# A node table stored twice with a mate mark, a shorter search, a later bias and a fuller tail in a four-layer graph kernel

## What is computed

```python
x = x + gnn0(layernorm(x), adj)      # bilinear attention in each graph, masked by adj, then elu
x = x + ffn0(layernorm(x))           # top-1 of 8 experts, 128 -> 512 -> 128, with a capacity per expert
x = x + gnn1(layernorm(x), adj)      # additive attention in each graph, out = attn @ hidden + bias
x = x + ffn1(layernorm(x), edges)    # GAT over the edges picks 2 of 4 experts per token
```

```python
h = (x_flat @ W_gat).reshape(M, HEADS, NUM_EXPERTS)       # 16 numbers per node
a_src, a_dst = (h * att_src).sum(-1), (h * att_dst).sum(-1)
e = leaky_relu(a_src[src] + a_dst[dst])                   # one loop edge per node is added
alpha = softmax of e over the edges that end in dst
agg = segment_sum(h[src] * alpha, dst)                    # 16 numbers per node
scores = layernorm(agg + b).mean over heads; the two best of 4 gelu experts, weighted, give the result
```

## Time and profile before

| | us |
|---|---|
| three runs of the kernel | 3044.87, 3047.87, 3049.06 (median 3047.87) |
| profiled execution, its own time | 3049.74 |
| its span (first to last instruction) | 3047.3 |

### The profile page before, as it was taken

One profiled execution on the slowest core, in us unless ns is written; L12 is line 12 of the kernel. 1 busy time (PEld: TensorE's weight loads), 2 busy tenths in 40 slices (PEclk: granted clock), 3 DMA queues, 4 the chain that ended last, 5 costly groups with the idle time before them and its releaser, 6 DMA issues. The chain is left out here.

```text
span 3047.3 us, 31102 instructions
## 1 busy us (share of the span) xinstructions
PE 1772.2 (58%) x8831; PEld 1216.7 (40%) x8831; DVE 2258.0 (74%) x4431; ACT 1155.4 (38%) x2319; POOL 1867.5 (61%) x1723
## 2 busy tenths in 40 slices
PE   0776774068787883566963356455545554555545
PEld 0565653045555552355761133233323332333223
DVE  7999998889999999777843655665566556655566
ACT  2676773234444441365941222222222222222222
POOL 4703244835454553477767777777777777777771
PEclk9998895589999997688956677677777777777777
DMA  5698000111111100222121122112211222122211
GB/s 217 210 354 323 16 23 15 33 38 35 35 44 42 53 27 35 71 58 69 34 41 29 39 45 43 33 41 45 43 37 36 45 43 41 35 43 45 43 31 36
DMA packets 170129, 192.34 MB, mean 63 GB/s; under 512 B 59241, under 2 KB 126096, under 8 KB 169008
## 3 DMA queue, kind: packets, MB, share of 16 engines
q1 hardware_dynamic: 107616, 118.69, 11.7%
q0 software_dynamic: 57088, 62.48, 10.1%
q10 hardware_dynamic: 5328, 9.97, 0.9%
HBM read 91.70 MB, written 105.25 MB: 65 GB/s over the span
## 5 line engine op out<-in xcount | busy, mean ns | idle before, releaser
L1582 POOL DMA_INDIRECT edge_rows<-node_table,edge_ids x1024 | 999.3, 976 | 313.2 <-issue 296.5
L1207 POOL DMA_INDIRECT token_results<-arena,token_of x160 | 255.4, 1596 | 293.4 <-ACT arena L1141 220.7
L634 DVE TENSOR_TENSOR sort_ping<-sort_pong 128x1024 f32<-128x1024 f32 (+1 forms) x232 | 395.2, 1745 | 6.0 <-ACT sort_pong L1077 1.1
L634 DVE TENSOR_TENSOR sort_pong<-sort_ping 128x1024 f32<-128x1024 f32 (+1 forms) x230 | 390.2, 1738 | 10.9 <-ACT sort_ping L1077 6.0
L1705 PE MATMUL x_b_featT<-ident,x_feat 128*128 128x128 f32 x128 | 34.8, 427 | 620.1 <-PEq L1304 620.1
L1200 POOL DMA_INDIRECT slots<-arena,send x128 | 190.0, 1485 | 301.9 <-ACT arena L1099 268.0
L1452 DVE TENSOR_TENSOR win_score<-win,masked 128x320 f32<-128x320 f32 x64 | 28.7, 490 | 446.3 <-DMA win<-edge_table,win_ids 445.1
L1711 PE MATMUL x_b_hid<-x_featT,x_w 128*128 128x512 f32 x512 | 312.2, 765 | 28.1 <-PEq L1304 28.1
L1718 PEld LDWEIGHTS x_b_res<-x_w,x_hid 128*128 128x128 f32 x2048 | 247.0, 197 | 97.5 <-issue 97.5
L1705 PEld LDWEIGHTS x_b_featT<-ident,x_feat 128*128 128x128 f32 x128 | 22.9, 217 | 625.4 <-issue 625.4
L1718 PE MATMUL x_b_res<-x_w,x_hid 128*128 128x128 f32 x2048 | 272.1, 288 | 0.0
(11 more groups left out here) (367 smaller groups left out, 4060.7 us busy)
## 6 DMA issues: line engine op xcount, KB each, us to landing
edge_table<-zeros SPq DMA_DIRECT2D x8, 5120.0 KB, 36.0
edge_rows<-node_table,edge_ids POOLq DMA_INDIRECT x1024
arena<-slots SPq DMA_DIRECT2D x40, 260.0 KB, 2.6
slots<-zeros SPq DMA_DIRECT2D x2, 5120.0 KB, 24.4
edge_table<-edge_rows SPq DMA_DIRECT2D x64, 160.0 KB, 2.1
out_dram<-x_y ACTq DMA_DIRECT2D x33, 256.0 KB, 4.1
x<-in_x_dram SPq DMA_DIRECT2D x4, 2048.0 KB, 16.7
adjacent<-in_adj_dram SPq DMA_DIRECT2D x32, 256.0 KB, 2.7
```

The source lines that it names most:

```text
L634: step(dve.tensor_tensor(vb[:, :, t, :], va[:, :, 0, :], va[:, :, 1, :], op))
L1207: pool.indirect_dma_start(rows_dram, bass.IndirectOffsetOnAxis(token_of[:, n % 4, r:r + 1], 0), res[:, n % 2, r, :], None, bounds_check=TO ...
L1582: pool.indirect_dma_start(rows[:, u, c, :], None, table_dram, bass.IndirectOffsetOnAxis(ids[:, u, c:c + 1], 0)).then_inc(rows_in[u], 16)
```

## The change

1. **Node table twice.** `node_table` has 2 x 16384 rows of 21 floats (`EDGE_ROW`; 84 B) in place of 16384 rows of 24 (96 B). Column 20 (`MATE_AT`) is 0 in the first copy and 1 in the second; it is filled, row by row, by two DMAs of SP behind the clears, which write whole rows of `zeros` and of a new tile `second_row`. The ids of the edges' sources keep the mate bit of the key (mask `MATES * NODE_BIT - 1`), so that an edge of the second mate fetches its source's row from the second copy, and carries the mark into `edge_table` (now 21 floats a row, cleared in pieces of 672 floats).
2. **The store of the table.** Each of the four stores L961 becomes two, one per copy, of 128 x 32 x 20 floats; SP waits for eight.
3. **A quarter of the search goes.** Of 32 searches, the 8 that looked up the second mate's first edge are left out (`SEARCHED`): 192 instead of 256 indirect DMAs on POOL, 24 instead of 32 pairs of operations on DVE. The 24 stand where the loop's 24 stood before; the searches behind the loop are gone. What is left of either mate's run is now counted from the pair's first edge (`pair_degree`).
4. **Hiding by the mark.** In each of the 32 turns the single operation on `hide` (L1458) becomes two on as many elements (a maximum, and a comparison with a maximum) that read the mark from the window.
5. **Later bias.** `dve_biased` stands at the head of GNN1's iteration, for n+2, where it stood behind the scores, for n+3.
6. **Fuller tail.** The condition on `advance()` in the tail of GNN0 goes, so the iterations 34, 36 and 38 take one step of the sort each, too.

```diff
+MATE_AT = ROW
+EDGE_ROW = ROW + 1
...
+CLEAR_EDGES = 32 * EDGE_ROW
...
-        zeros = sb("zeros", [P, CLEAR])
+        zeros, second_row = sb("zeros", [P, CLEAR_EDGES]), sb("second_row", [P, EDGE_ROW])
...
+        EACH = ALL_PAIRS // SEARCH
+        SEARCHED = [n for n in range(SEARCHES // SEARCH) if n // EACH != 2]
...
                     place(LAST_OF.index(n - 2))
-                if n <= GROUPS + 1 or n % 2:
-                    advance(2 if n > GATED and n % 2 == 0 and n <= GROUPS else 1)
+                advance(2 if n > GATED and n % 2 == 0 and n <= GROUPS else 1)
                 att0.dve_updated(dve, n - 1)
...
-                cols = slice(n * SEARCH, (n + 1) * SEARCH)
+                cols = slice(SEARCHED[n] * SEARCH, (SEARCHED[n] + 1) * SEARCH)
...
             for n in range(-3, GROUPS + 1):
+                att1.dve_biased(dve, n + 2)
                 att1.dve_held(dve, n - 1)
                 att1.dve_scores(dve, n + 2)
-                att1.dve_biased(dve, n + 3)
                 att1.dve_updated(dve, n - 1)
...
-                    link(dve.tensor_scalar(tiles_u, table[:, :].bitcast(U32), NODE_BIT - 1, None, ALU.bitwise_and))
+                    link(dve.tensor_scalar(tiles_u, table[:, :].bitcast(U32), MATES * NODE_BIT - 1, None, ALU.bitwise_and))
...
             for n in range(GROUPS + 1 - LAG, GROUPS):
                 gat.dve(dve, n)
-                if n % 3 == 0:
-                    search()
-            while searched[0] < SEARCHES // SEARCH:
+            while searched[0] < len(SEARCHED):
                 search()
...
-            clear(sp, edges_dram, cleared)
+            clear(sp, edges_dram, cleared, CLEAR_EDGES)
...
+            for mate, row in enumerate((zeros[:, 0:EDGE_ROW], second_row[:, :])):
+                copy_v = table_dram[mate * TOKENS:(mate + 1) * TOKENS, :].rearrange("(p r) c -> p r c", p=P)
+                sp.dma_start(copy_v, row.unsqueeze(1).to_broadcast([P, GRAPHS, EDGE_ROW])).then_inc(cleared, 16)
...
                 sp.wait_ge(gat.kept, (c + 1) * CHUNK)
-                sp.dma_start(table_v[:, cols, :], tab[:, cols, :]).then_inc(tabled, 16)
-            sp.wait_ge(tabled, 16 * (GROUPS // CHUNK))
+                for mate in range(MATES):
+                    sp.dma_start(table_v[mate][:, cols, 0:ROW], tab[:, cols, 0:ROW]).then_inc(tabled, 16)
+            sp.wait_ge(tabled, 16 * MATES * (GROUPS // CHUNK))
...
-            link(dve.tensor_tensor(by_mate(left[:, 0:GRAPHS], 0), by_unit(second_of[:, 0:ALL_PAIRS]), by_unit(first_edge), ALU.subtract))
-            link(dve.tensor_copy(by_mate(left[:, 0:GRAPHS], 1), by_unit(pair_degree[:, :])))
+            for mate in range(MATES):
+                link(dve.tensor_copy(by_mate(left[:, 0:GRAPHS], mate), by_unit(pair_degree[:, :])))
...
+            second = w[:, :, :, MATE_AT]
...
-                step(dve.scalar_tensor_tensor(hide[:, PAIRS:UNIT, :], hide[:, PAIRS:UNIT, :], 1.0, hide[:, 0:PAIRS, :], ALU.add, ALU.subtract))
+                step(dve.tensor_tensor(hide[:, 0:PAIRS, :], hide[:, 0:PAIRS, :], second, ALU.max))
+                step(dve.scalar_tensor_tensor(hide[:, PAIRS:UNIT, :], second, 0.5, hide[:, PAIRS:UNIT, :], ALU.is_lt, ALU.max))
...
-    table_dram = nc.dram_tensor("node_table", (TOKENS, TAB), F32).ap()
+    table_dram = nc.dram_tensor("node_table", (MATES * TOKENS, EDGE_ROW), F32).ap()
...
-    edges_dram = nc.dram_tensor("edge_table", (BLOCKS_MAX * BLOCK, ROW), F32).ap()
+    edges_dram = nc.dram_tensor("edge_table", (BLOCKS_MAX * BLOCK, EDGE_ROW), F32).ap()
```

More of the change, by code:

```diff
@@ L595, in front, with clears, clear @@
                      (spread_a, NODE_BIT << 16), (spread_b, 3 * NODE_BIT << LOG_NODES))
-        def clears(table):
-            return -(-(math.prod(table.shape) // P) // (CLEAR * REPEAT))
-        def clear(sp, table, done):
+        def clears(table, run=CLEAR):
+            return -(-(math.prod(table.shape) // P) // (run * REPEAT))
+        def clear(sp, table, done, run=CLEAR):
             flat = table.rearrange("(p r) d -> p (r d)", p=P)
-            width = math.gcd(flat.shape[1], CLEAR)
-            for c in range(clears(table)):
-                part = flat[:, c * CLEAR * REPEAT:min((c + 1) * CLEAR * REPEAT, flat.shape[1])].rearrange("p (r w) -> p r w", w=width)
+            width = math.gcd(flat.shape[1], run)
+            for c in range(clears(table, run)):
+                part = flat[:, c * run * REPEAT:min((c + 1) * run * REPEAT, flat.shape[1])].rearrange("p (r w) -> p r w", w=width)
                 sp.dma_start(part, zeros[:, 0:width].unsqueeze(1).to_broadcast(list(part.shape))).then_inc(done, 16)
@@ L931, in _ @@
                 sp.dma_start(adjacent[:, c % ADJ_SLOTS, :], a["adj"][:, c * WIDE:(c + 1) * WIDE]).then_inc(adj_in[c % ADJ_SLOTS], 16)
-            sp.wait_ge(zeroed, 1)
+            sp.wait_ge(zeroed, 3)
             clear(sp, slots_dram, slots_clear)
             clear(sp, rows_dram, unwritten)
-            clear(sp, edges_dram, cleared)
+            clear(sp, edges_dram, cleared, CLEAR_EDGES)
             ids_tail = ids_dram[P:, :].rearrange("r (p f) -> (r p) f", f=4 * PART_TILES)
             sp.dma_start(ids_tail, zeros[:, 0:4 * PART_TILES].bitcast(U32)).then_inc(cleared, 16)
+            for mate, row in enumerate((zeros[:, 0:EDGE_ROW], second_row[:, :])):
+                copy_v = table_dram[mate * TOKENS:(mate + 1) * TOKENS, :].rearrange("(p r) c -> p r c", p=P)
+                sp.dma_start(copy_v, row.unsqueeze(1).to_broadcast([P, GRAPHS, EDGE_ROW])).then_inc(cleared, 16)
             for s in sent:
@@ L955, in _ @@
             sp.wait_ge(ids_out, 16)
-            sp.wait_ge(cleared, clears(edges_dram) * 16 + 16)
-            table_v = table_dram.rearrange("(b i) c -> i b c", i=NODES)
+            sp.wait_ge(cleared, clears(edges_dram, CLEAR_EDGES) * 16 + 16 + 16 * MATES)
+            table_v = [table_dram[mate * TOKENS:(mate + 1) * TOKENS, :].rearrange("(b i) c -> i b c", i=NODES) for mate in range(MATES)]
             for c in range(GROUPS // CHUNK):
@@ L1171, in _ @@
             pool.memset(zeros[:, :], 0.0).then_inc(zeroed, 1)
+            pool.memset(second_row[:, 0:MATE_AT], 0.0).then_inc(zeroed, 1)
+            pool.memset(second_row[:, MATE_AT:EDGE_ROW], 1.0).then_inc(zeroed, 1)
             flat = masked[:, :, :].rearrange("p b j -> p (b j)")
@@ L1214, in _ @@
             pool.wait_ge(ranked_s, 1)
-            for n in range(SEARCHES // SEARCH):
+            for n, group in enumerate(SEARCHED):
                 ge(pool, looked, n - FETCHED + 1)
                 for c in range(SEARCH):
-                    q = n * SEARCH + c
+                    q = group * SEARCH + c
                     pool.indirect_dma_start(fetched[n % FETCHED][:, c, :], None, keys_dram,
@@ L1247, in edges_and_experts1 @@
         first_edge = found[:, 0, 0:ALL_PAIRS]
-        last_node = sb("last_node", [P, TAB])
-        ids, rows = sb("edge_ids", [P, 2, PART_TILES], U32), sb("edge_rows", [P, 2, PART_TILES, ROW])
-        win, win_ids = sb("win", [P, PAIRS, WINDOW * ROW]), sb("win_ids", [P, PAIRS], U32)
+        last_node = sb("last_node", [P, EDGE_ROW])
+        ids, rows = sb("edge_ids", [P, 2, PART_TILES], U32), sb("edge_rows", [P, 2, PART_TILES, EDGE_ROW])
+        win, win_ids = sb("win", [P, PAIRS, WINDOW * EDGE_ROW]), sb("win_ids", [P, PAIRS], U32)
         top, total, acc = sb("top", [P, GRAPHS, HEADS]), sb("total", [P, GRAPHS, HEADS]), sb("acc", [P, GRAPHS, GAT])
@@ L1416, in _ @@
             FULL, HALF_FULL = [P, UNIT, WINDOW, HEADS], [P, PAIRS, WINDOW, HEADS]
-            w = win[:, :, :].rearrange("p t (k c) -> p t k c", c=ROW)
-            w_flat = win[:, :, :].rearrange("p t (k c) -> p (t k) c", c=ROW)
+            w = win[:, :, :].rearrange("p t (k c) -> p t k c", c=EDGE_ROW)
+            w_flat = win[:, :, :].rearrange("p t (k c) -> p (t k) c", c=EDGE_ROW)
+            second = w[:, :, :, MATE_AT]
             flat = sc[:, :, :, :].rearrange("p t k h -> p (t k h)")
@@ L1618, in _ @@
                 sp.dma_start(ids[:, u, :], ids_v[u]).then_inc(ids_in[u], 16)
-            sp.dma_start(last_node[:, :], bass.AP(table_dram.tensor, (TOKENS - 1) * TAB, [[0, P], [1, TAB]])).then_inc(consts_in, 16)
+            sp.dma_start(last_node[:, :], bass.AP(table_dram.tensor, (TOKENS - 1) * EDGE_ROW, [[0, P], [1, EDGE_ROW]])).then_inc(consts_in, 16)
             for to, of in ((gat_b, "gat_b"), (gamma, "gamma"), (beta, "beta")):
```

## The result

The change made the kernel slower, by 0.55%. Five runs took 3062.32 to 3069.27 us, median 3065.08, against a median of 3048.08 before; the ratio is 1.0055 (95% interval 1.0044 to 1.0065). The profiled execution took 3062.68 us, with a span of 3061.0. In a later series the same kernel took 3055.83 us against 3047.23, a ratio of 1.0037 (1.0023 to 1.0050); that series stands with the experiments. The forecast was 3042.8 us, and the range ended at 3055.

What follows compares the result with a forecast made beforehand. POOL's 1024 gathers were taken to bound the last stage, a PE-DVE round trip the GNN1 loop. Terms -14 + 6.4 + 2 + 0.5 = -5.1 us on 3049.74 gave 3044.6, or 3042.8 us for a median; range 3028 to 3055.

Steps and rivals of the forecast that it cites:

- The store: End of the front: two last DMAs instead of one land 5.6 to 10.4 us behind the last projected row; +2 us.
- The fills: Two DMAs behind the clears, near 280 us: at most 42 us of DMA, hidden, so 0.
- The cover: Nothing asks for the filled rows before 1465 us, so their DMA time is hidden; without it, 42 us.
- The fuller tail: GNN0's tail: three more sort steps on DVE slow POOL's scatters, so the experts start later; +6.4 us, bounds 0 and +10.
- The later bias: GNN1 loop: DVE's bias no longer waits for PE's hidden; half of 27.3 us is gained, -14 us.
- rival C: GNN1 loop: the bias's wait moves to the scores, only 5 us gained; 3051.8 us in all, chance 0.11.
- Rival A: GNN1 loop: the whole bias wait of 27.3 us goes; 3029.5 us in all, chance 0.20.
- The last turns: Last stage: DVE's added operation per turn shows only in the two turns behind the last gather; +0.5 us.
- the case that the marks are paid in full: Last stage: DVE's added 0.23 us operation is hidden in none of the 32 turns; +7.5 us.
- Rival B: Last stage, L1582: gathers of 84 B rows from two copies take longer; 20 ns each gives 3063 us; chance 0.10.

Runs made afterwards that it cites:

- the last two experiments: Changed kernel with 96 B pitch, no fuller tail and six-part table store: 3033.93 us with the later bias, 3049.09 us with the bias at its old place.

## Why the prediction was wrong

- *The store, +2 us (bounds -0.5 and +4.3)*: this is the step that failed. It took for each of the new pieces, 80 B at a pitch of 84, the landing of the old ones, 96 B at a pitch of 96, and noted the difference in length without pricing it. By it both copies would have landed 5.6 to 10.4 us behind the last row; the last one landed 21.0 us behind it in the first profile, 19.0 in the later series and 12.8 at a pitch of 96 B. Measured from the last row to the last stage the term is +13.5 us in the first profile, +11.5 in the later series (1598.35 - 1577.04 = 21.3 against 9.8). Even at 96 B it was +5.3, a microsecond above the upper bound; the pitch made the rest.
- *The fills, 0, at most 42 us of DMA*: with rows of 96 B the price was near (46.4 us), with those of 84 B they took 131. The cover had a hole that the prediction did not name: the scatters land later beside the fills, and ACT waits for them. 0 to 2 us of it came through in the medians, some 5 in the first profile.
- *The fuller tail, +6.4*: right in place and sign; 7.1 us at the scatters' end, 7.8 at the first turn, 4.8 to 8.4 in the medians.
- *The later bias, -14*: right in size. From the first turn to the last row it took 909.1 to 914.9 us in the thirteen profiles with the later bias (mean 912.8), 925.6 to 928.3 in the four with the old one (mean 927.0), some 14 us by the last two experiments, too. The mechanism was only half right, so the size is in part luck: the part of the wait that remained did not appear at the scores (8.5 - 5.1 = 3.4 us of rival C) but for the most part at the GAT's projections (26.9 - 7.9 = 19.0 us), which no rival named. Rival A's 27.3 us did not come about. What the working had not seen either is that the whole gain needs the quarter of the search gone: alone the bias gave 8 us.
- *The last turns, +0.5*: not visible; from the last gather's start to the end 60.1 us, before 60.5. But the last stage as a whole is some 5 us longer with two copies, within the 7.5 us that the prediction gave for the case that the marks are paid in full; whether the marks make it is not shown.
- *Rival B*, slower by longer gathers, had the right suspect, the rows of 84 B, in the wrong place: the pitch of 84 B costs the gathers nothing (mean 975 to 979 ns at 84 B, 978 to 980 at 96 and 128), but it makes the writing slow. Some 4 ns a gather did come, with two copies at any pitch. The range was too narrow because its slower side hung on the reading alone.

With the measured terms the sum is -15.8 + 7.8 + 13.5 + 1 (fills) = +6.5 us, and +11.5 with the last stage's 5; the later series has +8.6. The first profiled execution was 3062.68 - 3049.74 = 12.9 us above its counterpart. The 6.4 us between that and 6.5 are the first turn at 673.9 us, which two profiles of the same kernel did not repeat; the most of it was lost beside the fills. The direction, slower, does not hang on it.

## What to carry to other kernels

Price a DMA of many small pieces by a row of the trace with the same pitch, or measure it: a table whose rows were narrowed from 96 to 84 B took 1.6 times as long to store and 2.8 times as long to fill as at 96 B, and the time of a gather did not change with the pitch. Where a front ends with a store, cut the last part small, and look at what runs beside it, since of a gain of 14 us upstream only 8 showed until the search that ended beside it was shortened too. A hole on an engine that nobody waits for is not free: the work put into it slowed another engine that did set the end.

## What was not expected of the hardware

- Two fills of 16384 pieces each had landed 130.5 us after the second's issue at 84 B a piece and pitch, and 46.4 us at 96 B, with more bytes in the second case; one copy's stores of 92 B delayed the last stage by 3.7 us against 96 B.
- Of the eight stores, issued in pairs, the first of each pair took SP 0.36 us to issue and the second 2.9 to 3.1, at 96 B 2.9, too; each of the four single ones took 0.36.
- Scatters that POOL issues landed late while fills of 84 B pieces ran: ACT waited 9.8 to 16.2 us for them, and not at all with fills in pieces of 96 or 128 B, or of 168 and 2688 B.
- The first work of the last stage came 11.7 us behind POOL's last fetch in the kernel before and 11.3 us in the later bias alone, though a fetch lands after 2.4 us in the median; behind a landed store it came after 2.3 us. What fills the rest is open.
